# The last expert layer reordered and its group 3 split, with 32 fewer matmuls of ones in the last attention

## What is computed

```python
# attention 3: 16 heads of 8, self and auxiliary keys, two softmaxes, gated sum
dots, dots_aux = q @ k.T * scale, q @ ka.T * scale
out = softmax(dots) @ v * (1 - gate) + softmax(dots_aux) @ va * gate
x = x + tanh(g_xattn[3]) * (out @ Wo + bo)
# experts 3: 32 experts x 4 sets; groups of 32 tokens; each expert takes the best token of a group
logits = einsum('bgtd,des->bgtes', grouped, controller) + tie
perm = (logits == max(logits, axis=t))
dispatched = einsum('bgtd,bgtes->bgesd', grouped, perm)
inner = relu(einsum('bgesd,desf->bgesf', dispatched, f1) + bias)
intermediate = einsum('bgesf,esfd->bgesd', inner, f2)
x = x + tanh(g_ffn[3]) * einsum('bgesd,bgtes->bgtd', intermediate, perm)
```

## Time and profile before

| | us |
|---|---|
| median of 3 runs | 674.17 (672.97 to 679.03) |
| profiled execution | 677.38 |
| its span, first to last instruction | 675.6 |
| PE busy in it | 600.6 (89%) |
| DVE busy | 427.7 (63%) |
| ACT busy | 316.6 (47%) |
| POOL busy | 212.5 (31%) |
| mean granted PE clock | 0.959 of 2.4 GHz |

### The profile page before, as it was taken

How to read it: one execution, slowest core, us unless ns; L and a number is a source line. 1 busy time by engine, 2 the same in 40 slices (tenths; PEclk the granted TensorE clock), 3 DMA queues, 4 the chain that set the end, 5 groups by cost and what they waited for, 6 DMA issues and landing times.

```text
span 675.6 us, 14842 instructions
## 1 busy us (share of the span) xinstructions
PE 600.6 (89%) x5760; PEld 397.3 (59%) x5761; DVE 427.7 (63%) x1240; ACT 316.6 (47%) x706; POOL 212.5 (31%) x412
## 2 busy tenths in 40 slices
PE   6899999999998799846689899989999988899688
PEld 6666666666655488532456365554556665566474
DVE  3457678787787421778988776436656767763543
ACT  2544536345352244355633223212666776676244
POOL 2043433445445535630021252532243352120000
PEclk9999999999999799878879899989999999999999
DMA  9781000000000344200000125104003040002101
GB/s 291 180 266 31 1 1 1 1 9 9 1 8 9 92 126 117 70 1 0 1 0 1 38 60 132 48 0 120 13 7 105 6 108 6 5 8 67 61 4 63
DMA packets 34183, 34.94 MB, mean 52 GB/s; under 512 B 8794, under 2 KB 29826, under 8 KB 33666
## 3 DMA queue, kind: packets, MB, share of 16 engines
q1 hardware_dynamic: 31648, 31.41, 16.3%
q0 software_dynamic: 1024, 2.11, 0.9%
q10 hardware_dynamic: 1442, 0.48, 0.3%
HBM read 20.02 MB, written 5.26 MB: 37 GB/s over the span
## 4 chain that ended last, share of the span: by engine, by line
PE 66%; DVE 16%; issue 6%; ACT 5%; POOL 5%; DMA 2%; POOLq 0%; DVEq 0%; ACTq 0%; SPq 0%
PE bank L600 5%; PE bank L1722 5%; PE bank L2078 5%; PE bank L524 4%; PE bank L556 4%; PE bank L533 4%; PE bank L2093 4%; PE bank L453 4%; PE bank L1781 3%; POOL y_tokens L1240 2%; PE bank L543 2%; PE bank L568 2%; PE bank L2128 2%; PE bank L2137 2%; PE bank L2628 1%
## 5 line engine op out<-in xcount | busy, mean ns | idle before, releaser
L2314 DVE TENSOR_REDUCE mx<-bank 128x4 f32<-128x512 f32 (+1 forms) x128 | 73.2, 581 | 42.3 <-PE bank L2086 40.8
L2407 ACT ACTIVATE area_a<-bank 128x512 f32<-128x512 f32 (+1 forms) x128 | 74.4, 596 | 47.9 <-PE bank L2093 46.5
L955 ACT ACTIVATE area_a<-bank,beta 128x154 f32<-128x154 f32 x128 | 42.0, 412 | 77.3 <-PE bank L524 77.1
L453 PE MATMUL bank<-ones_b 128*128 128x512 bf16 x176 | 56.9, 419 | 2.4 <-DVE X L1881 0.9
L1043 POOL TENSOR_TENSOR area_a<-area_a,rs 128x512 f32<-128x512 f32 (+1 forms) x48 | 40.8, 878 | 50.7 <-DVE rs L759 50.7
L600 PEld LDWEIGHTS bank<-area_a 128*128 128x128 f32 x320 | 39.6, 191 | 18.4 <-ACT area_a L948 9.7
L600 PE MATMUL bank<-area_a 128*128 128x128 f32 x320 | 46.4, 285 | 0.0
L524 PE MATMUL bank<-ctx_flat,area_a 128*128 128x154 f32 x256 | 43.8, 307 | 0.0
L524 PEld LDWEIGHTS bank<-ctx_flat,area_a 128*128 128x128 f32 x256 | 38.4, 199 | 7.9 <-issue 7.3
L556 PE MATMUL bank<-area_a,xnT 128*128 128x512 f32 (+1 forms) x96 | 41.7, 515 | 0.0
L1722 PE MATMUL bank<-area_a 128*128 128x512 f32 x80 | 39.9, 626 | 0.0
(11 more groups left out here) (368 smaller groups left out, 1447.5 us busy)
## 6 DMA issues: line engine op xcount, KB each, us to landing
area_a<-xn_area SPq DMA_DIRECT2D x48, 128.0 KB, 2.5
area_b<-in_w SPq DMA_DIRECT2D x16, 256.0 KB, 4.8
f<-in_f SPq DMA_DIRECT2D x1, 2048.0 KB
area_a<-in_f SPq DMA_DIRECT2D x1, 2048.0 KB, 8.6
area_b<-xn_area SPq DMA_DIRECT2D x6, 308.0 KB, 5.4
area_a<-in_rows SPq DMA_DIRECT2D x10, 128.0 KB, 2.7
x_slots<-xn_area SPq DMA_DIRECT2D x1, 1032.0 KB, 7.9
area_a<-x_slots SPq DMA_DIRECT2D x8, 129.0 KB, 2.2
```

The lines of the kernel that those rows point to most:

```text
L453: pe.matmul(psum[:, 0:n], ones_b[:, :], ones_b[:, :].unsqueeze(1).to_broadcast([128, n // 128, 128]), start=True, stop=True)
L955: m = act.activation(kk0[:, g % 2, h, :], src[:, (h - lo) * 2 * T:(h - lo + 1) * 2 * T], ACT.Identity, bias=beta0[:, h:h + 1])
L2314: dve.tensor_reduce(mx3[:, b % 2, aux, heads3(half, 1 - odd)], SCORES_RING3[j % 2][:, 0:4 * n].rearrange("p (h k) -> p h k", k=n), AX.X, A ...
L2407: act.activation((ea3 if aux else em3)[:, heads3(half, odd), :], EXP_RING3[j % 2][0:T if aux else 128, :].rearrange("p (h q) -> p h q", q= ...
```

## The change

- Ones in the attention: two for b = -2 and -1, one for b = 0, none for b = 1 to 3.
- Group 3 is routed in two pieces, tiles 0 to 2 (`lo = 0, hi = 3`) and tile 3 (`lo = 3, hi = 4`). POOL's reciprocal deviations, the norms, transposes and logits of tiles 0 to 2 stand in b = 16 of the attention; the copies of gather 0 move behind the outputs of tile 15. Tile 3's transposes and logits use bank 4 (`MISC3`).
- Gathers write other banks (`D_BANK[g]`, `D_LAST`), and wait for the count of copies that frees those (`D_COPIES`); copies are issued singly.
- The experts run first 0 to 3, then second 0 to 3, whose banks alternate between 0 to 3 and 4 to 7; second(1) waits for all biases, since it overwrites the banks of the first matmuls.
- The matmuls of ones of `tensor_moe3` are placed anew: 14 before; 6 between the gathers and four behind the third eviction after.

```diff
--- before.py
+++ after.py
@@ -2006,44 +2006,51 @@
                 m = pe.matmul(PREP3[:, :], wqk3[:, kind - 1, :], xnT4[:, n % 2, :], start=True, stop=True)
             m.then_inc(prep3_in_psum, 1)
 
-        D_BANK = bank[0:4]
-
-        def tensor_norms_turned3(pe, g):
+        D_BANK = [[bank[n] for n in places] for places in ((0, 1, 2, 3), (6, 0, 7, 2), (1, 6, 3, 7), (0, 1, 2, 3))]
+        D_COPIES = (0, 1, 3, 5)
+        D_LAST = (bank[5], bank[6], bank[4], bank[7])
+
+        def prep_view(lo):
+
+            return MISC3 if lo == 3 else PREP3
+
+        def tensor_norms_turned3(pe, g, lo=0, hi=4):
             if g == 0:
                 pe.wait_ge(prep3_done, block3(3, V3))
             elif g == 1:
                 pe.wait_ge(perm3_done, 1)
             else:
                 pe.wait_ge(pt3_done, g)
-            pe.wait_ge(g_xn_done, 4 * (g + 17))
-            for j in range(4):
-                m = pe.transpose(PREP3[:, j * 128:(j + 1) * 128], XN3[g][:, j, :], ident[:, :])
+            pe.wait_ge(g_xn_done, 4 * (g + 16) + hi)
+            for j in range(lo, hi):
+                m = pe.transpose(prep_view(lo)[:, j * 128:(j + 1) * 128], XN3[g][:, j, :], ident[:, :])
             m.then_inc(g_xnT_in_psum, 1)
 
-        def tensor_expert_logits3(pe, g):
-            pe.wait_ge(g_xnT_done, g + 17)
-            pe.matmul(PREP3[:, :], ctrl3[:, :], xnT4[:, g % 2, :], start=True, stop=True).then_inc(l3_in_psum, 1)
-
-        def tensor_choice_turned3(pe, g):
-            pe.wait_ge(perm3_done, max(g + 1, 2))
+        def tensor_expert_logits3(pe, g, lo=0, hi=4):
+            pe.wait_ge(g_xnT_done, g + 17 + lo // 3)
+            pe.matmul(prep_view(lo)[:, lo * 128:hi * 128], ctrl3[:, :], xnT4[:, g % 2, lo * 128:hi * 128], start=True, stop=True).then_inc(l3_in_psum, 1)
+
+        def tensor_choice_turned3(pe, g, lo=0, hi=4):
+            pe.wait_ge(perm3_done, max(g + 1, 2) + lo // 3)
             at_least(pe, pt3_done, g)
-            for j in range(4):
+            for j in range(lo, hi):
                 tok = (4 * g + j) * 128
-                m = pe.transpose(PREP3[:, j * 128:(j + 1) * 128], perm3[:, tok:tok + 128], ident[:, :])
+                m = pe.transpose(prep_view(lo)[:, j * 128:(j + 1) * 128], perm3[:, tok:tok + 128], ident[:, :])
             m.then_inc(pt3_in_psum, 1)
 
-        def tensor_gather3(pe, g):
-            pe.wait_ge(pt3_done, g + 1)
+        def tensor_gather3(pe, g, lo=0, hi=4):
+            pe.wait_ge(pt3_done, g + 1 + lo // 3)
             if g == 0:
                 pe.wait_ge(max3_done, 8 * B)
                 pe.wait_ge(exp3_done, 8 * B)
             else:
-                pe.wait_ge(d3_dve_done, 2 * g)
-                pe.wait_ge(d3_act_done, 2 * g)
-            for j in range(4):
+                pe.wait_ge(d3_dve_done, D_COPIES[g])
+                pe.wait_ge(d3_act_done, D_COPIES[g])
+            for j in range(lo, hi):
                 for r in range(4):
                     p = slice(G3 * r, G3 * r + G3)
-                    m = pe.matmul(D_BANK[r][:, j::4], XN3[g][p, j, :], PT3[g][p, j, :], start=True, stop=True)
+                    out = D_LAST[r][:, 0:128] if lo == 3 else D_BANK[g][r][:, j::4]
+                    m = pe.matmul(out, XN3[g][p, j, :], PT3[g][p, j, :], start=True, stop=True)
             m.then_inc(d3_in_psum, 1)
 
         def tensor_ahead3(pe, b, j):
@@ -2068,6 +2075,10 @@
                 tensor_choice_turned3(pe, 2)
             if (b, j) == (16, 1):
                 tensor_gather3(pe, 0)
+            if (b, j) == (16, 3):
+                tensor_norms_turned3(pe, 3, 0, 3)
+            if (b, j) == (16, 7):
+                tensor_expert_logits3(pe, 3, 0, 3)
 
         def tensor_attn3(pe):
             def sums(b, aux, i):
@@ -2098,8 +2109,8 @@
                 shifted, ahead = b >= 0, b + 2 < B
                 if ahead:
                     at_least(pe, max3_done, 8 * (b + 2) + j - 1)
-                    if b < 4:
-                        keep_busy(pe, SCORES_RING3[j % 2], 2 if b <= 0 else 1)
+                    if b < 1:
+                        keep_busy(pe, SCORES_RING3[j % 2], 2 if b < 0 else 1)
                 if shifted:
                     at_least(pe, exp3_done, 8 * b + j - 1)
                 if not ahead and j % 2 == 0:
@@ -2241,6 +2252,8 @@
             if j == 0:
                 dve.wait_ge(g_rstd_done, 21 + g)
                 dve.wait_ge(g_xnT_in_psum, 15 + g)
+            if (g, j) == (3, 3):
+                dve.wait_ge(g_rstd_done, 25)
             dve.tensor_scalar(XN3[g][:, j, :], X[:, 4 * g + j, :], g_mv[:, g, j, 0:1], g_rstd[:, g, j:j + 1],
                               ALU.subtract, ALU.mult).then_inc(g_xn_done, 1)
 
@@ -2249,23 +2262,28 @@
             best, n = gmax3[:, 4 * lo:4 * hi], 4 * (hi - lo)
             dve.wait_ge(vector_step, vector_steps[0])
             if step == 0:
-                dve.wait_ge(l3_in_psum, g + 1)
-                m = dve.tensor_tensor(lt, PREP3[:, lo * 128:hi * 128].rearrange("p (g t) -> p g t", t=G3), tie3[:, :].unsqueeze(1).to_broadcast([128, n, G3]), ALU.add)
+                dve.wait_ge(l3_in_psum, g + 1 + lo // 3)
+                m = dve.tensor_tensor(lt, (MISC3 if lo == 3 else PREP3)[:, lo * 128:hi * 128].rearrange("p (g t) -> p g t", t=G3), tie3[:, :].unsqueeze(1).to_broadcast([128, n, G3]), ALU.add)
             if step == 1:
                 m = dve.tensor_reduce(best, lt, AX.X, ALU.max)
             if step == 2:
                 m = dve.tensor_tensor(perm3[:, g * 512 + lo * 128:g * 512 + hi * 128].rearrange("p (g t) -> p g t", t=G3), lt,
                                       best.unsqueeze(2).to_broadcast([128, n, G3]), ALU.is_equal)
-            if step == 2 and hi == 4:
+            if step == 2 and hi >= 3:
                 m.then_inc(perm3_done, 1)
             else:
                 m.then_inc(vector_step, 1)
                 vector_steps[0] += 1
 
-        def vector_gathered3(dve, g):
-            dve.wait_ge(d3_in_psum, g + 1)
-            for r in (2, 3):
-                dve.tensor_copy(d3_view(g, r), D_BANK[r][:, :].rearrange("p (e j) -> p e j", j=4)).then_inc(d3_dve_done, 1)
...
+        def vector_gathered3(dve, g, r, lo=0, hi=4):
+            dve.wait_ge(d3_in_psum, g + 1 + lo // 3)
+            dve.tensor_copy(d3_view(g, r, lo, hi), gathered_view(g, r, lo, hi)).then_inc(d3_dve_done, 1)
 
         def vector_ahead3(dve, b, j):
             if b in (6, 9, 13):
@@ -2302,7 +2320,11 @@
                 vector_tile_stats3(dve, 3, 2)
                 for u in range(3):
                     vector_tile_moments3(dve, 3, u)
-                vector_gathered3(dve, 0)
+                for u in range(3):
+                    vector_tile_norm3(dve, 3, u)
+            if (b, j) == (16, 5):
+                vector_gathered3(dve, 0, 2)
+                vector_gathered3(dve, 0, 3)
 
         def vector_attn3(dve):
             def maxima(b, j):
@@ -2370,15 +2392,18 @@
                 at_least(act, pool3_done, halves3(g - 1, kind) if g >= 1 else 0)
                 act.activation(tmp512[:, kind - 1, :], PREP3[:, :], ACT.Identity, bias=b3c[:, kind - 1:kind]).then_inc(prep3_done, 1)
 
-        def scalar_choice3(act, g):
-            act.wait_ge(pt3_in_psum, g + 1)
+        def scalar_norms_turned3(act, lo, hi):
+            act.wait_ge(g_xnT_in_psum, 20 + lo // 3)
+            act.activation(xnT4[:, 1, lo * 128:hi * 128], prep_view(lo)[:, lo * 128:hi * 128], ACT.Copy).then_inc(g_xnT_done, 1)
+
+        def scalar_choice3(act, g, lo=0, hi=4):
+            act.wait_ge(pt3_in_psum, g + 1 + lo // 3)
             at_least(act, d3_in_psum, g - 2)
-            act.activation(PT3[g].rearrange("p j e -> p (j e)"), PREP3[:, :], ACT.Copy).then_inc(pt3_done, 1)
-
-        def scalar_gathered3(act, g):
-            act.wait_ge(d3_in_psum, g + 1)
-            for r in (0, 1):
-                act.activation(d3_view(g, r), D_BANK[r][:, :].rearrange("p (e j) -> p e j", j=4), ACT.Copy).then_inc(d3_act_done, 1)
+            act.activation(PT3[g][:, lo:hi, :].rearrange("p j e -> p (j e)"), prep_view(lo)[:, lo * 128:hi * 128], ACT.Copy).then_inc(pt3_done, 1)
+
+        def scalar_gathered3(act, g, r, lo=0, hi=4):
+            act.wait_ge(d3_in_psum, g + 1 + lo // 3)
+            act.activation(d3_view(g, r, lo, hi), gathered_view(g, r, lo, hi), ACT.Copy).then_inc(d3_act_done, 1)
 
         def scalar_ahead3(act, b, j):
             if (b, j) == (10, 1):
@@ -2394,7 +2419,10 @@
             if (b, j) == (15, 7):
                 scalar_choice3(act, 2)
             if (b, j) == (16, 2):
-                scalar_gathered3(act, 0)
+                scalar_gathered3(act, 0, 0)
+                scalar_gathered3(act, 0, 1)
+            if (b, j) == (16, 5):
+                scalar_norms_turned3(act, 0, 3)
 
         def scalar_attn3(act):
             def exps(b, j):
@@ -2480,6 +2508,11 @@
             pool.wait_ge(g_xn_done, 4 * (12 + g + 1))
```

(103 more changed lines are left out.)

23 lines of the change are left out of this document (12 added, 11 removed).

## The result

Twenty runs of each: before 674.19 us median (670.86 to 680.52), after **670.0** (660.48 to 675.92); the ratio is 0.9836 (95% interval 0.9801 to 0.9871), 11 us. The medians of all runs are only 4.2 us apart, the means 6.7, the fastest runs 10.4; after's times run with the granted clock of the execution (0.963 to 0.969 in its six fastest, 0.941 to 0.951 in its eight slowest). The forecast was 13.6 us. The profiled execution after took 671.32 us (span 669.5), 6.1 us of span less than the one before.

A forecast was written before the change was run, and what follows sets the result against it. PE bound the attention and last stage, hand-offs the routing, eviction waits part of the expert matmuls. Gains 6.55 + 4.35 + 1.5 + 1.2 = 13.6 us off the 674.17 median gave 660.6 us, range 657.5 to 666.0.

The forecast's parts named there:

- the first rival: Half rate finds another place, such as the sparse routing: last-stage gain lost and one further spell, 663.0 us; chance 18%.
- part 4: Last stage: matmuls and four ones ahead shorten PE's idle time, so the half-rate spell vanishes, 1.2 us (bounds 0 and 1.5).
- part 3: Expert matmuls: all first, then all second, hides evictions except the last; 15.0 to 13.5 us, gain 1.5 (bounds 0.8, 1.8).
- Part 1: Attention b=0 to 3: 32 fewer ones, all on the path; 5.25 + 1.3 = 6.55 us (bounds 5.0 and 7.0).
- the price of the cover: Attention: ones also keep the clock up; charged nothing for removing them, as b=5 to 7 ran at 1.00 without any.
- Part 2: Group 3's routing: tiles 0 to 2 go ahead of tile 15's update; first expert matmul 4.35 us earlier (bounds 2.5, 5.3).
- half rate finds another place: Sparse routing or elsewhere: spells of 3 us cost 1.2 to 1.5 each; time 663.0 us, chance 18%.
- Attention gives it back: Attention: loads of maximum rows or stacks, or POOL's splits, end last; ones worth only 1.5, 665.6 us; chance 11%.
- the chain is longer: Routing: PE waits in order for a copy behind a smaller step; 2 us less gain, 662.6 us; chance 12%.
- The clock of the thinned tiles: Attention's first tiles: without ones the clock falls to half, b=1 to 3 doubles, 688 us; chance 4%.

The follow-up runs named there:

- routing and experts alone: The changed kernel with the removed attention ones put back, so only routing and expert order differ from before: 674.9 us median, ratio 0.9973.
- six ones: The changed kernel plus six matmuls of ones in b=11 before PE's wait for group 1's norms: 667.46 us (ratio 0.9848), again 667.22 us (0.9843).
- both kernels with only the ones thinned: Kernel before without the 32 attention ones: 679.25 us, ratio 1.0063; the same plus six ones before b=11's wait: 677.21 us, ratio 0.9979.
- four against twelve ones: Four ones ahead of the pauses, added to the kernel with six ones: 666.79 us; twelve ones among the changed kernel's first matmuls: 673.2 us.

## Why the prediction was right, and where it was not

- **The time.** By the ratio the gain is 11 us (663.1 from 674.17), 2.5 short of the forecast and inside its range of 657.5 to 666.0. By the medians of all runs it is 4.2, and 670.0 lies outside the range. The two profiled executions differ by 6.1 us of span. So the forecast fits the faster half of after's runs, and there partly by luck: of its four parts one had the wrong sign in the trace, and a cost of 3.9 us at b=11 was not in it. That 663.1 is the 663.0 of the first rival is chance too, since that sum left part 4 out and kept part 3 whole.
- **Part 1, the ones: right in the attention.** 6.54 us against 6.55. For b=1 to b=3 the counterpart in b=5 to b=7 gave the price to the hundredth, and a kernel with the ones put back took the old 31.37 us. What the step left out is the price of the cover. It was put at nothing because the clock stayed at 1.00 in b=5 to b=7, and it did stay in b=0 to b=4. It fell eight tiles on. A second price was not thought of: with the ones thinned, the expert matmuls take 1.3 to 1.7 us more, in either order.
- **Part 2, the routing: right in its steps, low by 0.55.** 4.9 us (4.7 and 0.2) against 4.35. The output matmul came 0.2 earlier, as said. POOL's power took 0.85 (0.86 said), DVE's steps 0.54 and 0.28 (0.55 and 0.3). The rest must lie in the hand-offs, which were not taken apart.
- **Part 3, the expert order: the step that failed.** 13.5 us forecast, 16.26 measured, so a loss of 1.26 instead of a gain of 1.5. The step took PE's 11.99 us of work as free to stand in one block. The evictions do hide, and the last one is the 1.49 assumed. But PE ran out of instructions: two pauses, 3.04 us. Before had no such pause to warn of it: its waits lay where two of the pauses would be, and the first stands only in kernels with the thinned ones. The order itself is not what lost: beside a kernel with the same ones, it won some 0.4 us together with the routing (14.64 against 14.99, 16.26 against 16.64), not 1.5.
- **Part 4, the last stage: right.** 651.13 to 669.5 is 18.37 us, before 19.85, so 1.48 against 1.2; its transposes take 0.66 us from the start. Other traces agree: with the four ones ahead and full clock behind them it takes 18.4 us (after, routing and experts alone, six ones), with the old wait of 1.5 us 19.6 to 19.9 (before, both kernels with only the ones thinned).
- **The rival "half rate finds another place" took place** beside the four parts, at b=11 and, in other executions, in the expert matmuls. It was priced too low: 1.2 to 1.5 us for one stretch of about 3 us, where the stretch of 10.2 us at b=11 cost 3.6 and one of 13.7 over the second matmuls 5.1. Against it I had set that the equally sparse routing kept its clock; that was the wrong place to look, since b=11 had kept its own in before as well.
- **Attention gives it back, the chain is longer:** neither. **The clock of the thinned tiles:** it stayed at 1.00; the rule of the Trainium skill (TensorE: Matmul & The Clock Gate) would have made it 688. What it says of gaps agrees in kind, in another place and size than I gave it: in seven traces the low clock comes behind a later wait of 1.4 us, in three others it doesn't.
- **Open:** why the parts don't add up in the median. Thinning alone lost 4.8 us, the routing and the expert order alone won nothing sure, both together 4.4. The profiles point to half rate that falls into the expert layer, but one execution of each is too few to say how often, and those of the two partial kernels were their fastest runs. Open too is what sends the first instruction block's packet, and with it why the thinned ones bring the first pause, and what decides whether the wait at b=11 costs the clock.

## What to carry to other kernels

Price a removed filler twice: by its own counterpart in the trace, and by every wait of the engine further on, where the clock may fall; then look at the scatter of the runs, not only at the median. When a reordering packs short instructions into one run, count instructions as well as microseconds: here 256 of them can't be had in less than 3.5 us, and waits that look like waste may be hiding just that. Taking instructions out far ahead moves every later block too, so compare the pauses with all other parts of the change held fixed before blaming one of them. Filler put in that gap is free, filler beside it is not (four against twelve ones).

## What the runs showed of the hardware

- Among the expert matmuls one block of 256 instructions reached PE per 3.5 to 3.8 us (once 4.0), and in fourteen traces no two of its packets started less than 3.4 us apart; 128 pairs of weight load and small matmul run in 2.0 us, so such work is bound by its instructions, and 128 pairs less saved 3.34 us.
- Once at half rate, TensorE stayed there for 13.7 and 17.1 us over unbroken small matmuls (12.64 and 13.03 us for 256 that take 7.54), where at b=11 four of the seven stretches lasted 3.4 us and three 10.2.
- The same 1.40 us wait was followed by half rate, 1.5 to 1.9 us behind its end, in seven of eight traces with the thinned ones, and in neither of the two with all of them; filled with six ones it wasn't in four of four. What decides is not shown.
- A matmul of ones of 512 columns cost 0.22 us in the attention, but 0.44 us each where twelve of them broke up the small first matmuls.
